# One subtraction of 2048 columns for the low part of a block of adj in the last pass, in place of two of 1024

## The chip, the core and the metric

The kernel runs on one core of a Trainium2 chip. The time is that of the device for one execution, in microseconds (us). The core's engines that matter here are TensorE (PE in the profile; PEld is its weight load), VectorE (DVE), ScalarE (ACT), and SyncE (SP), whose queue issues the transfers. Each engine works through its own instructions in the order in which they are written, and waits on semaphores that other engines raise.

## The reference

A graph network over 4096 nodes with 128 features each, and one 4096 x 4096 matrix `adj` that serves as every adjacency matrix:

```python
x = layernorm(x + relu(adj @ x @ kernel + bias))
u, v = x, v_node_feats
for _ in range(3):
    v = mlp(adj @ u, uv weights)      # three 128 x 128 layers with leaky_relu
    u = mlp(adj @ v, vu weights)
return layernorm(x + v)
```

So `adj` is multiplied with a 4096 x 128 matrix six times (the last `u` isn't used): six passes, each dependent on the one before. All of it is float32.

## The kernel before

`adj` (64 MB) doesn't fit on the chip and is read from memory again and again, in blocks of 512 x 512, that is 128 partitions x 2048 columns, 1 MB each. A block is used for the pass at hand ("finish") and, where the order allows it, for the start of the next pass too ("begin"), so passes 0 to 4 use most blocks twice. The last pass has nothing to begin: its 36 blocks are used once each, which makes it the stretch with the most loads for each product.

Precision comes from splitting. A float32 operand is written as a high part (rounded to the matmul's float32 format) and a low part (what is left), and a product is made of three matmuls: high x high, low x high, high x low. For each block of `adj`:

- SyncE loads it in two halves of 1024 columns (512 KB each) into `adj_raw`, a ring of 8 halves. It may load half h only when VectorE has finished with half h-8 (the wait on `adj_lo_ready` in `block.sync`, L492 issues the load).
- ScalarE copies each half to the high part (L613) as soon as TensorE has used up the block that lay in the target's place. There are 4 places in `adj_hi`/`adj_lo`, and in the last pass 2 more in the feature buffers that are no longer needed (`feat_hi`/`feat_lo` in the profile's rows at L613 and L742 are those).
- VectorE subtracts the high part from the raw half and writes the low part (L742), with one increment of `adj_lo_ready` a half.
- TensorE uses them: L878 (high x high), L885 (low features), L892 (low part of adj), 12 matmuls of 512 columns a block. The very last block has its own lines, L866 to L869.

Between these run the steps of the small network (MLP) of each finished group of 512 nodes, a "unit". In the last pass, for the row r of blocks that has just been finished: VectorE adds the two partial sums (`part`, L731), TensorE multiplies by the first weights (L825; L828 where nothing is to be added), ScalarE applies leaky_relu (`hid`, L507), TensorE the second layer (L811), ScalarE again, TensorE the third (L789), VectorE adds the bias (`pre`, L709), ScalarE applies leaky_relu (`post`, L507), and the normalisation follows: VectorE sum with x (L690), statistics (L626, L630), ScalarE square root (`std`, L538), VectorE reciprocal and shift (L665, L667), ScalarE the result (`resid`, L528), SyncE the store. Hidden layers in passes before the last one are split in high and low parts too (`in_lo` L722, `hid_lo` L717; TensorE L750 to L752).

The order of everything is fixed ahead of time by `Plan`, in ticks of one 128-column tile of a block (three matmuls). `steps` gives each MLP step its tick, `due` gives each half of a block the tick at which ScalarE and VectorE turn to it, in the last pass 20 ticks ahead of its use. In one tick an engine first issues the MLP steps and then the halves that are due. The rows of the last pass are done in the order 7, 0, 6, 5, 4, 3, 1, 2.

Of the kernel before, what the change touches and what calls it, by code (L numbers as in the profile page):

```python
# [4 lines left out]
F32 = mybir.dt.float32  # L5
F32R = mybir.dt.float32r
ALU = mybir.AluOpType
# [3 lines left out]
CHUNK = 512  # L11
# [6 lines left out]
PASSES = 6  # L18
RING = 4
SPARE = 2  # L20
RAW = 8
# [100 lines left out]
class Plan:  # L122
# [90 lines left out]
    def pieces_before(self, b, pieces):  # L213

        return TILES if b in self.first_spare else pieces

    def first_use(self, b):
        return next(n for n, of in enumerate(self.block) if of == b)
# [17 lines left out]
    def kind_of(self, u):  # L236
        return KINDS[self.units[u][0]]
# [42 lines left out]
def gnn_kernel(nc, x, adj, weights, bias_rows, out):  # L280
    C = x.shape[0]
    plan = Plan(C)
# [10 lines left out]
    with ctx:  # L293
        def sb(name, shape, dt=F32):
            return ctx.enter_context(nc.sbuf_tensor(name, shape, dt))
# [4 lines left out]
        def sem(name):  # L300
            return ctx.enter_context(nc.semaphore(name))

        adj_raw = sb("adj_raw", [P, RAW, HALF])
# [42 lines left out]
        adj_hi_ready = sem("adj_hi_ready")  # L346
        adj_lo_ready = sem("adj_lo_ready")
# [44 lines left out]
        def columns(chunk):  # L392
            return slice(chunk * CHUNK, (chunk + 1) * CHUNK)
# [61 lines left out]
        def split_block(adj, feat, b):  # L455

            k = plan.slot[b]
            return adj[:, k, :] if k < RING else feat[PASSES % 2][:, (k - RING) * BLOCK:(k - RING + 1) * BLOCK]

        def split_hi(b):  # L460
            return split_block(adj_hi, feat_hi, b)

        def split_lo(b):
            return split_block(adj_lo, feat_lo, b)
# [40 lines left out]
        def _(act):  # L505
# [7 lines left out]
            for t in range(plan.ticks + TAIL):  # L513
# [77 lines left out]
                if g is not None:  # L591
                    s, _, r = plan.groups[g]
                    act.wait_ge(half_used, plan.pieces_of(plan.closes[g]))
                    of = plan.unit_of(s, r)
                    if s and plan.summed(of):
                        if plan.in_parts(of):
                            act.wait_ge(in_lo_ready, plan.count_in_parts(of))
                        else:
                            act.wait_ge(hid1_done, deep(of) + 1)
                    act.activation(part_of(plan.node(s, r)), group_bank(g), ACT.Copy).then_inc(part_kept, 1)  # L600
# [17 lines left out]
        def _(dve):  # L618
# [26 lines left out]
            h = 0  # L645
            for t in range(plan.ticks + TAIL):
# [55 lines left out]
                if u is not None:  # L702
                    b = OUT_BIAS[kind_of(u)]
# [29 lines left out]
                while h < len(plan.loads) and plan.due[h] <= t:  # L733
                    b, i, pieces = plan.loads[h]
                    if b in plan.brings_x and i == 0:
                        c = plan.brings_x[b]
                        dve.wait_ge(x_hi_ready, plan.xs.index(c) + 1)
                        dve.tensor_tensor(feat_lo[0][:, columns(c)], resid[:, columns(c)],
                                          feat_hi[0][:, columns(c)].bitcast(F32), ALU.subtract).then_inc(x_lo_ready, 1)
                    slot = slice(i * CHUNK, (i + pieces) * CHUNK)  # L740
                    dve.wait_ge(adj_hi_ready, h + 1)
                    dve.tensor_tensor(split_lo(b)[:, slot], adj_raw[:, h % RAW, 0:pieces * CHUNK],  # L742
                                      split_hi(b)[:, slot].bitcast(F32), ALU.subtract).then_inc(adj_lo_ready, 1)
                    h += 1

        @block.tensor
        def _(pe):
# [173 lines left out]
```

## Time and profile before

| | us |
|---|---|
| median of three runs | 1170.84 (1170.68 to 1171.25) |
| the profiled execution | 1170.68 |
| its span, first to last instruction | 1168.8 |
| TensorE busy | 1154.0 (99%) |
| VectorE busy | 738.1 (63%) |
| ScalarE busy | 660.9 (57%) |
| L742 on VectorE, 488 halves | 577.0 |

The span is 1.9 us less than the time of the same execution. TensorE's granted clock is 0.999 over the span. In the page's 40 slices TensorE is at 9 tenths from the second to the last but one. VectorE is at 4 to 6 tenths in the middle and at 6 to 8 tenths in the last five, which are the last pass. An instruction's row gives its start and its duration. Where an engine stood idle before it, square brackets name for how long and who ended it. Two VectorE or ScalarE instructions in a row overlap in these rows by about 0.09 us, so the second starts a little before the first one's end.

### The profile page before, as it was taken

To read this page: it belongs to the slowest core of one execution; us is meant where nothing else is said; L and a number is where in the kernel's file an instruction comes from. 1 tells how busy PE (TensorE), PEld (TensorE's weight loads), DVE (VectorE), ACT (ScalarE), POOL (GpSimd) and SP (SyncE) were. 2 spreads that over 40 slices of the span, in tenths; PEclk is the share of its full clock that TensorE was granted. 3 is DMA by queue.
4 is the path that set the end of the run, shared out by engine and by line. 5 is a ranking of instruction groups with operands and counts; after the bars stand their busy time and mean duration, and the time that the engine had idled before them with its cause. 6 is when DMAs were issued, how large, how long until landed. Compare 5 with 4: busy or idle time off the path is not lost.

```text
span 1168.8 us, 13697 instructions
## 1 busy us (share of the span) xinstructions
PE 1154.0 (99%) x5236; PEld 953.2 (82%) x5236; DVE 738.1 (63%) x890; ACT 660.9 (57%) x809; POOL 0.2 (0%) x4
## 2 busy tenths in 40 slices
PE   7999999999999999999999999999999999999997
PEld 6888888888888888888888888888888888887776
DVE  7997676458564555555545746554566555678884
ACT  7765555346554555555444754554556444667874
POOL 0000000000000000000000000000000000000000
PEclk9999999999999999999999999999999999999999
DMA  9988785568366646555656736655665555589870
GB/s 383 406 302 321 247 271 191 206 215 288 125 205 210 216 161 224 189 184 180 216 180 216 250 116 223 207 179 178 207 225 184 195 200 214 188 296 362 297 261 36
DMA packets 72209, 261.60 MB, mean 224 GB/s; under 512 B 8016, under 2 KB 8656, under 8 KB 71120
## 3 DMA queue, kind: packets, MB, share of 16 engines
q1 hardware_dynamic: 72000, 260.61, 63.6%
q8 instruction: 41, 0.67, 0.2%
q14 instruction: 24, 0.20, 0.0%
q10 hardware_dynamic: 144, 0.13, 0.0%
HBM read 258.61 MB, written 2.10 MB: 223 GB/s over the span
## 4 chain that ended last, share of the span: by engine, by line
PE 93%; DMA 3%; DVE 2%; ACT 1%; issue 0%; SPq 0%; DVEq 0%; ACTq 0%
PE agg_ps L892 28%; PE agg_ps L885 28%; PE agg_ps L878 28%; PE pre_ps L789 4%; DMA adj_raw<-in_adj 3%; PE hid_ps L750 1%; PE hid_ps L752 1%; PE hid_ps L751 1%; DVE adj_lo L742 1%; ACT adj_hi L613 1%; PE hid_ps L811 1%; PE hid_ps L825 0%; ACT feat_hi L613 0%; DVE stats L626 0%; ACT resid L528 0%
## 5 line engine op out<-in xcount | busy, mean ns | idle before, releaser
L742 DVE TENSOR_TENSOR adj_lo<-adj_raw,adj_hi 128x1024 fp32r<-128x1024 f32 x464 | 548.1, 1221 | 226.4 <-ACT adj_hi L613 221.0
L878 PE MATMUL agg_ps<-adj_hi,feat_hi 128*128 128x512 f32 x1484 | 587.0, 396 | 7.5 <-ACT adj_hi L613 7.5
L885 PE MATMUL agg_ps<-adj_hi,feat_lo 128*128 128x512 f32 x1484 | 579.4, 390 | 0.0
L613 ACT ACTIVATE adj_hi<-adj_raw 128x1024 fp32r<-128x1024 f32 x464 | 468.3, 1052 | 86.0 <-PE agg_ps L892 72.4
L892 PE MATMUL agg_ps<-adj_lo,feat_hi 128*128 128x512 f32 x1484 | 458.8, 390 | 0.2 <-DVE adj_lo L742 0.2
L878 PEld LDWEIGHTS agg_ps<-adj_hi,feat_hi 128*128 128x128 f32 x1484 | 279.6, 188 | 66.4 <-issue 9.8
L885 PEld LDWEIGHTS agg_ps<-adj_hi,feat_lo 128*128 128x128 f32 x1484 | 279.5, 188 | 59.7 <-issue 2.4
L892 PEld LDWEIGHTS agg_ps<-adj_lo,feat_hi 128*128 128x128 f32 x1484 | 278.9, 188 | 59.6 <-DVE adj_lo L742 1.1
L507 ACT ACTIVATE hid<-hid_ps,params 128x512 f32<-128x512 f32 (+1 forms) x80 | 54.5, 681 | 61.0 <-PE hid_ps L752 50.6
L578 ACT ACTIVATE in_hi<-part 128x512 fp32r<-128x512 f32 x24 | 15.2, 634 | 110.4 <-DVE part L731 110.4
L507 ACT ACTIVATE post<-pre 128x512 f32<-128x512 f32 x39 | 24.6, 631 | 79.8 <-DVE pre L709 79.8
L709 DVE TENSOR_TENSOR pre<-pre_ps,b_row 128x512 f32<-128x512 f32 x47 | 32.4, 690 | 55.5 <-PE pre_ps L789 55.5
L731 DVE TENSOR_TENSOR part<-part,agg_ps 128x512 f32<-128x512 f32 (+1 forms) x31 | 20.6, 666 | 66.7 <-PE agg_ps L892 65.0
L789 PEld LDWEIGHTS pre_ps<-params,hid 128*128 128x128 f32 x380 | 49.9, 191 | 4.0
L789 PE MATMUL pre_ps<-params,hid 128*128 128x128 f32 x380 | 50.3, 275 | 0.0
L600 ACT ACTIVATE part<-agg_ps 128x512 f32<-128x512 f32 x30 | 17.9, 597 | 25.6 <-PE agg_ps L892 22.3
L742 DVE TENSOR_TENSOR feat_lo<-adj_raw,feat_hi 128x1024 fp32r<-128x1024 f32 x24 | 28.9, 1223 | 4.5 <-ACT feat_hi L613 4.1
L613 ACT ACTIVATE feat_hi<-adj_raw 128x1024 fp32r<-128x1024 f32 x24 | 24.8, 1056 | 9.0 <-PE agg_ps L892 8.9
L717 DVE TENSOR_TENSOR hid_lo<-hid,hid_hi 128x512 fp32r<-128x512 f32 x32 | 22.0, 687 | 11.9 <-ACT hid L507 11.9
L578 ACT ACTIVATE in_hi<-agg_ps 128x512 fp32r<-128x512 f32 x8 | 4.8, 598 | 41.5 <-PE agg_ps L892 41.5
L507 ACT ACTIVATE hid_hi<-hid_ps,params 128x512 fp32r<-128x512 f32 x32 | 21.9, 684 | 10.6 <-PE hid_ps L752 10.6
L722 DVE TENSOR_TENSOR in_lo<-agg_ps,in_hi 128x512 fp32r<-128x512 f32 x8 | 5.5, 691 | 35.2 <-ACT in_hi L578 35.2
(78 smaller groups left out, 382.3 us busy)
## 6 DMA issues: line engine op xcount, KB each, us to landing
adj_raw<-in_adj SPq DMA_DIRECT2D x472, 512.0 KB, 5.6
adj_raw<-in_adj SPq DMA_DIRECT2D x8, 1024.0 KB, 8.1
resid<-in_x SPq DMA_DIRECT2D x8, 256.0 KB, 8.1
out<-resid SPq DMA_DIRECT2D x7, 256.0 KB, 5.5
params<-in_weights SPq DMA_DIRECT2D x1, 386.0 KB, 4.7
b_row<-in_bias_rows SPq DMA_DIRECT2D x1, 128.0 KB, 5.6
out<-resid ACTq DMA_DIRECT2D x1, 128.0 KB, 2.1
out<-resid SPq DMA_DIRECT2D x1, 128.0 KB, 2.2
```

What stands on the lines that cost most here:

```text
L507: return act.activation(to, of, ACT.Prelu, alpha=SLOPE, **bias)
L578: act.activation(in_hi[:, :], agg(u), ACT.Copy).then_inc(in_hi_ready, 1)
L600: act.activation(part_of(plan.node(s, r)), group_bank(g), ACT.Copy).then_inc(part_kept, 1)
L613: act.activation(split_hi(b)[:, i * CHUNK:(i + pieces) * CHUNK], adj_raw[:, h % RAW, 0:pieces * CHUNK], ACT.Copy).then_inc(adj_hi_ready, 1)
L709: dve.tensor_tensor(by_tile(pre[:, own(u)]), by_tile(layer_bank(2, u)), b_row[:, b * P:(b + 1) * P].rearrange("p (j f) -> p j f", f=P) .to ...
L717: dve.tensor_tensor(hid_lo[:, :], hid1[:, :], hid_hi[:, :].bitcast(F32), ALU.subtract)\
L731: dve.tensor_tensor(agg(u), agg(u), agg_bank(u), ALU.add).then_inc(sum_kept, 1)
L742: dve.tensor_tensor(split_lo(b)[:, slot], adj_raw[:, h % RAW, 0:pieces * CHUNK], split_hi(b)[:, slot].bitcast(F32), ALU.subtract).then_inc ...
L789: last = pe.matmul(layer_bank(2, u)[:, k * P:(k + 1) * P], hid2[:, j * P:(j + 1) * P], w_raw[:, OUT_W[kind_of(u)], :], start=not biased, s ...
L878: pe.matmul(group_bank(g), feat_hi[feats][:, tile(src, i)], split_hi(b)[:, piece(i)], start=start, stop=False)
L885: pe.matmul(group_bank(g), feat_lo[feats][:, tile(src, i)], split_hi(b)[:, piece(i)], start=False, stop=False)
L892: last = pe.matmul(group_bank(g), feat_hi[feats][:, tile(src, k)], split_lo(b)[:, piece(k)], start=False, stop=stop and k == i)
```

## The change

In the last pass (blocks whose first use is in pass 5, 36 of them) VectorE does nothing at a block's first half. At the second half it waits until both high parts are there and makes the low part of the whole block in one subtraction of 2048 columns, and then raises `adj_lo_ready` by 2. Both raw halves lie side by side in the ring. Blocks of passes 0 to 4 are done as before, in two subtractions. ScalarE's, TensorE's and SyncE's programs are the same as before.

```diff
+    def low_at_once(self, b):
+        return self.order[self.first_use(b)][0] == PASSES - 1
...
+                    h += 1
+                    if plan.low_at_once(b):
+                        if i == 0:
+                            continue
+                        raw = adj_raw[:, (h - 2) % RAW:(h - 2) % RAW + 2, :].rearrange("p k f -> p (k f)")
+                        dve.wait_ge(adj_hi_ready, h)
+                        dve.tensor_tensor(split_lo(b), raw, split_hi(b).bitcast(F32), ALU.subtract)\
+                           .then_inc(adj_lo_ready, 2)
+                        continue
                     slot = slice(i * CHUNK, (i + pieces) * CHUNK)
-                    dve.wait_ge(adj_hi_ready, h + 1)
-                    dve.tensor_tensor(split_lo(b)[:, slot], adj_raw[:, h % RAW, 0:pieces * CHUNK],
+                    dve.wait_ge(adj_hi_ready, h)
+                    dve.tensor_tensor(split_lo(b)[:, slot], adj_raw[:, (h - 1) % RAW, 0:pieces * CHUNK],
                                       split_hi(b)[:, slot].bitcast(F32), ALU.subtract).then_inc(adj_lo_ready, 1)
-                    h += 1
```

VectorE's order at the turn of the passes, where the last unit of pass 4 goes through its MLP (`in_lo`, `hid_lo`), before:

```order
L722 TENSOR_TENSOR in_lo<-agg_ps,in_hi 128x512
L742 TENSOR_TENSOR adj_lo<-adj_raw,adj_hi 128x1024
L742 TENSOR_TENSOR feat_lo<-adj_raw,feat_hi 128x1024 x2
L717 TENSOR_TENSOR hid_lo<-hid,hid_hi 128x512
```

and after:

```order
L726 TENSOR_TENSOR in_lo<-agg_ps,in_hi 128x512
L750 TENSOR_TENSOR adj_lo<-adj_raw,adj_hi 128x2048
L750 TENSOR_TENSOR feat_lo<-adj_raw,feat_hi 128x2048
L721 TENSOR_TENSOR hid_lo<-hid,hid_hi 128x512
```

A first half that stood ahead of `in_lo` has moved behind it, so that four halves stand between `in_lo` and `hid_lo` in place of three.

VectorE's order where row 7's unit is normalised and row 6's sum follows (`post` to `part`), before:

```order
L709 TENSOR_TENSOR pre<-pre_ps,b_row 128x512
L742 TENSOR_TENSOR feat_lo<-adj_raw,feat_hi 128x1024
L742 TENSOR_TENSOR adj_lo<-adj_raw,adj_hi 128x1024
L690 TENSOR_TENSOR post<-post,resid 128x512
L626 BN_STATS stats<-post 128x6 x4
L630 BN_AGGR mean_var<-stats 128x2 x4
L742 TENSOR_TENSOR adj_lo<-adj_raw,adj_hi 128x1024 x2
L665 RECIPROCAL rstd<-std 128x4
L667 SCALAR_TENSOR_TENSOR shift<-mean_var,rstd 128x4
L742 TENSOR_TENSOR adj_lo<-adj_raw,adj_hi 128x1024
L731 TENSOR_TENSOR part<-part,agg_ps 128x512
```

and after:

```order
L713 TENSOR_TENSOR pre<-pre_ps,b_row 128x512
L750 TENSOR_TENSOR feat_lo<-adj_raw,feat_hi 128x2048
L694 TENSOR_TENSOR post<-post,resid 128x512
L630 BN_STATS stats<-post 128x6 x4
L634 BN_AGGR mean_var<-stats 128x2 x4
L750 TENSOR_TENSOR adj_lo<-adj_raw,adj_hi 128x2048
L669 RECIPROCAL rstd<-std 128x4
L671 SCALAR_TENSOR_TENSOR shift<-mean_var,rstd 128x4
L750 TENSOR_TENSOR adj_lo<-adj_raw,adj_hi 128x2048
L735 TENSOR_TENSOR part<-part,agg_ps 128x512
```

A first half that stood ahead of the sum with x (`post`) has moved behind the statistics.

VectorE's order where row 5's unit ends and row 4's sum follows, before:

```order
L709 TENSOR_TENSOR pre<-pre_ps,b_row 128x512
L742 TENSOR_TENSOR feat_lo<-adj_raw,feat_hi 128x1024 x2
L690 TENSOR_TENSOR post<-post,resid 128x512
L626 BN_STATS stats<-post 128x6 x4
L630 BN_AGGR mean_var<-stats 128x2 x4
L742 TENSOR_TENSOR adj_lo<-adj_raw,adj_hi 128x1024 x2
L665 RECIPROCAL rstd<-std 128x4
L667 SCALAR_TENSOR_TENSOR shift<-mean_var,rstd 128x4
L731 TENSOR_TENSOR part<-part,agg_ps 128x512
```

and after:

```order
L713 TENSOR_TENSOR pre<-pre_ps,b_row 128x512
L750 TENSOR_TENSOR feat_lo<-adj_raw,feat_hi 128x2048
L694 TENSOR_TENSOR post<-post,resid 128x512
L630 BN_STATS stats<-post 128x6 x4
L634 BN_AGGR mean_var<-stats 128x2 x4
L750 TENSOR_TENSOR adj_lo<-adj_raw,adj_hi 128x2048
L669 RECIPROCAL rstd<-std 128x4
L671 SCALAR_TENSOR_TENSOR shift<-mean_var,rstd 128x4
L735 TENSOR_TENSOR part<-part,agg_ps 128x512
```

Here every step keeps its place, and each pair of halves has become one instruction.

## Rows read from the trace of the kernel before

**Rows 1.** Busy time by stretch: PE, PEld, DVE, ACT, POOL, PEclk, DMA share, GB/s.

```profile
1040.00:1060.00 20.00, 20.00 (x93) 16.43 (x93) 19.16 (x18) 17.04 (x19) 0.00 (x0) 1.00 0.94 348
1100.00:1140.00 40.00, 39.80 (x176) 31.46 (x175) 35.78 (x53) 31.75 (x41) 0.00 (x0) 1.00 0.78 278
```

**Rows 2.** Group of L742 on the page: busy us, mean ns, idle before, releaser.

```profile
L742 DVE TENSOR_TENSOR adj_lo<-adj_raw,adj_hi 128x1024 fp32r<-128x1024 f32 x464 | 548.1, 1221 | 226.4 <-ACT adj_hi L613 221.0
```

**Rows 3.** Timeline of PE (start, duration, us): the last block's first matmul.

```profile
1155.63 0.28 PE L866 MATMUL agg_ps<-adj_hi,feat_hi 128*128 128x256 f32 x1
```

**Rows 4.** Timeline of all engines, turn of the passes.

```profile
1036.37 1.23 DVE L742 TENSOR_TENSOR adj_lo<-adj_raw,adj_hi 128x1024 fp32r<-128x1024 f32 x1 [0.26 <-ACT adj_hi L613]
...
1037.51 2.35 DVE L742 TENSOR_TENSOR feat_lo<-adj_raw,feat_hi 128x1024 fp32r<-128x1024 f32 x2
...
1040.43 0.69 DVE L717 TENSOR_TENSOR hid_lo<-hid,hid_hi 128x512 fp32r<-128x512 f32 x1 [0.57 <-ACT hid L507]
...
1041.27 0.47 PE L750 MATMUL hid_ps<-hid_hi,w_hi 128*128 128x512 f32 x1
```

**Rows 5.** Timeline of all engines, row 7's statistics and row 6's first layers.

```profile
1084.32 0.62 ACT L507 ACTIVATE post<-pre 128x512 f32<-128x512 f32 x1
1084.45 1.23 DVE L742 TENSOR_TENSOR adj_lo<-adj_raw,adj_hi 128x1024 fp32r<-128x1024 f32 x1 [1.26 <-ACT adj_hi L613]
...
1085.59 0.69 DVE L690 TENSOR_TENSOR post<-post,resid 128x512 f32<-128x512 f32 x1
...
1091.17 0.68 DVE L731 TENSOR_TENSOR part<-part,agg_ps 128x512 f32<-128x512 f32 x1
...
1092.00 1.10 PE L825 MATMUL hid_ps<-part,params 128*128 128x512 f32 x2 [0.35 <-DVE part L731]
...
1095.28 1.12 PE L811 MATMUL hid_ps<-hid,params 128*128 128x512 f32 x2 [0.34 <-ACT hid L507]
```

**Rows 6.** Timeline of all engines, row 5's second layer.

```profile
1113.26 0.66 ACT L507 ACTIVATE hid<-hid_ps,params 128x512 f32<-128x512 f32 x1
1114.43 1.02 PE L811 MATMUL hid_ps<-hid,params 128*128 128x512 f32 x2
```

**Rows 7.** Timeline of all engines, row 5's statistics and row 4's first layers.

```profile
1119.85 2.59 DVE L742 TENSOR_TENSOR feat_lo<-adj_raw,feat_hi 128x1024 fp32r<-128x1024 f32 x2 [0.45 <-ACT feat_hi L613]
...
1122.35 0.68 DVE L690 TENSOR_TENSOR post<-post,resid 128x512 f32<-128x512 f32 x1
...
1126.81 0.69 DVE L731 TENSOR_TENSOR part<-part,agg_ps 128x512 f32<-128x512 f32 x1
1126.92 1.65 ACT L528 ACTIVATE resid<-post,shift,rstd 128x128 f32<-128x128 f32 x4 [0.31 <-DVE shift L667]
...
1130.38 0.67 ACT L507 ACTIVATE hid<-hid_ps,params 128x512 f32<-128x512 f32 x1
...
1131.10 1.12 PE L811 MATMUL hid_ps<-hid,params 128*128 128x512 f32 x2 [0.20 <-ACT hid L507]
```

**Rows 8.** Timeline of all engines, row 4's statistics and row 3's first layer.

```profile
1138.01 1.22 DVE L742 TENSOR_TENSOR adj_lo<-adj_raw,adj_hi 128x1024 fp32r<-128x1024 f32 x1 [0.16 <-ACT adj_hi L613]
1139.16 0.69 DVE L690 TENSOR_TENSOR post<-post,resid 128x512 f32<-128x512 f32 x1
...
1141.08 0.65 DVE L731 TENSOR_TENSOR part<-part,agg_ps 128x512 f32<-128x512 f32 x1
...
1142.10 1.02 PE L825 MATMUL hid_ps<-part,params 128*128 128x512 f32 x2
```

**Rows 9.** Single loads and a split in the timelines of SP and ACT.

```profile
1033.12 0.33 SPq L492 DMA_DIRECT2D adj_raw<-in_adj  x1
...
1051.44 0.33 SPq L492 DMA_DIRECT2D adj_raw<-in_adj  x1
...
1059.12 1.06 ACT L613 ACTIVATE feat_hi<-adj_raw 128x1024 fp32r<-128x1024 f32 x1 [0.30 <-PE agg_ps L892]
```

**Rows 10.** All users of `adj_raw` from 1040 to 1060 us, its loads' landing times.

```profile
DMA to landing us min/median/max: 4.8/6.6/7.0
```

## The prediction

> **What bounds the kernel now.** I read the busy times by stretch first. TensorE is the engine at its limit. In the last pass it is busy 20.00 of 20 us and 39.80 of 40 us at a granted clock of 1.00, while VectorE has 19.16 of 20 and 35.78 of 40 [rows 1]. So any wait that is put on TensorE lengthens the run, since its matmuls come in a fixed order and none is skipped. A change on VectorE counts only where TensorE waits for it.
>
> Next comes the page's group for L742. A half takes 1221 ns, and VectorE idles 221 us in total before it until ScalarE's high part is there [rows 2]. VectorE is mostly ahead of its supply and not behind it.
>
> Then I looked at how early the low parts are. The last half starts at 1138.01 and ends at 1139.23 [rows 8], and TensorE takes up the last block at 1155.63 [rows 3]. That is 16.4 us of lead, so low parts that come one or two us later are not missed by the matmuls that read them.
>
> What has no such lead are the MLP steps. They stand in the same order on VectorE and ScalarE, behind the low parts. TensorE's waits in the last pass are all of that kind: 0.35 us for the sum `part`, 0.34 and 0.20 us for `hid` [rows 5, 7]. At other places the step comes only just in time.
>
> **The price of one merged subtraction.** 512 columns take 0.69 us (`hid_lo` [rows 4]) and 1024 take 1.22 us [rows 2], so 512 more cost 0.53 us and 2048 come to 1.22 + 2 x 0.53 = 2.28 us. Two halves in a row took 2.35 us [rows 4], so the second starts 2.35 - 1.22 = 1.13 us after the first. The next instruction starts about 0.09 us before the end of the one ahead. The merged one therefore holds VectorE for some 2.20 us, against 2 x 1.13 = 2.26 us. This saves about 0.06 us a block where both high parts are ready, or 36 x 0.06 = 2.2 us of VectorE's time in all. No row shows 2048 columns. If the fixed part were lost and only the data rate counted, it would be 2 x 1.07 = 2.14 us, and if nothing were saved 2.26 us. I take 2.20, which the two shapes give by a straight line.
>
> **What the merge delays.** Where VectorE waits for ScalarE, it did the first half while the second one's high part was still being made. Now it starts both when the second is ready. The step behind came 1.14 us after the second half's start (1138.01 to 1139.16 [rows 8]) and now comes 2.20 us after it, so it is 1.06 us late (0.99 to 1.12 with the bounds above). I followed this through each MLP unit between VectorE, ScalarE and TensorE.
>
> - Turn of the passes [rows 4]. The first merged one starts at 1036.37, the second at 1038.57, and `hid_lo` at 1040.77 in place of 1040.43. The gap of 0.57 us, in which it waited for ScalarE, covers the rest. `hid_lo` ended at 1041.12, and TensorE started L750 0.15 us later at 1041.27, so it has nothing in hand. TensorE: +0.34 us.
> - Row 6 [rows 5]. Here the order helps. The half at 1084.45 goes behind the statistics, and L690 can start once ScalarE's `post` is done, at 1084.32 + 0.62 = 1084.94, about 0.6 us earlier than 1085.59. Behind it stand two whole blocks in place of three halves, 2.20 - 1.13 = 1.07 us more. The sum `part` comes about 0.42 us later, and TensorE's wait of 0.35 us grows to 0.77. But ScalarE, which waited for the shift in this chain, is 0.6 us earlier, and with TensorE itself 0.42 us later the wait of 0.34 us at 1095.28 goes. Net: +0.08 us.
> - Row 5 [rows 6]. The same pattern as for row 4 in the next point. VectorE's shift is 1.02 us late, ScalarE waits for it, and its `hid` at 1113.26 comes 1.02 us late. From the start of such a `hid` to TensorE's start it takes 0.72 us (1130.38 to 1131.10 [rows 7]), so it was ready at 1113.98 for a matmul that went at 1114.43, with 0.45 us to spare. Net: +0.57 us.
> - Row 4 [rows 7]. Of the pair at 1119.85 the second half starts at 1119.85 + 2.59 - 1.23 = 1121.21. The merged one starts then, and L690 moves from 1122.35 to 1123.41. The next pair needs no wait and gives back about 0.04, so the shift is 1.02 us late. L528 had been waiting for that shift, 0.31 us. Everything behind it on ScalarE is back to back up to `hid` at 1130.38, for which TensorE already waited 0.20 us. Net: +1.02 us. The sum `part` is 1.02 us late as well, at 1126.81 + 0.69 + 1.02 + 0.15 = 1128.67 for L825. That lies in the same stretch of TensorE's order, ahead of L811, which now has to wait until 1132.12 anyway, so it adds nothing.
> - Row 3 [rows 8]. L690 and the sum `part` are 1.06 us late. `part` ended at 1141.73 and TensorE could have started 0.15 us later, as it did behind the `part` of [rows 5], at 1141.88. It started at 1142.10, so 0.22 us are to spare. Net: +0.84 us.
> - Rows 1 and 2 and the end: no low part is left behind 1139.23, and nothing changes but that all is shifted.
>
> Sum: 0.34 + 0.08 + 0.57 + 1.02 + 0.84 = 2.85 us, or 2.5 to 3.2 us with the merged one at its bounds. The delays add up, since ScalarE's splits wait for TensorE to free a place and so shift with it. The profiled execution took 1170.68 us with a span of 1168.8. It becomes 1173.5 us. The median of the runs is 0.16 us above it, which gives 1173.7. I forecast 1173.6.
>
> **The loads.** The raw halves come free later too, and SyncE's loads, which wait for them in order, start later. The worst is the half whose place let SyncE issue at 1033.12 [rows 9]. Its low part is now done at 1036.37 + 2.28 = 1038.65, and the load goes 5.5 us later, just ahead of the stretch in which the DMA engines are 94% busy [rows 1]. The load issued at 1051.44 is split at 1059.12, 7.68 us later, and the slowest of these lands in 7.0 [rows 9, 10]. So 0.7 us are to spare there, and 0.34 more since TensorE's shift moves the split. One lost transfer of 512 KB at 348 GB/s is 1.5 us. It uses up the spare and makes a few splits late by about half a us. These have the 16 us of lead above. I cost it at nothing, and if the MLP steps behind those splits are hit, at up to 1.5 us.
>
> **A rule that cuts both ways.** The rows show VectorE 89 to 96% busy in the last pass and yet waiting for ScalarE before several of its halves [rows 1, 4, 5, 7, 8]. The Trainium skill, Perfetto Trace Analysis, section "Optimizing Scalar/DVE Operations", says that larger operations help throughput if the engine is saturated, and that breaking instructions up may let work finish sooner where the engine isn't saturated but leaves bubbles on others. By its first half the change would gain, which is the second rival below. By its second half it would lose, as in my sum, and the brackets of the rows speak for that.
>
> **Rivals.**
>
> 1. VectorE counts as the bottleneck of the last pass, and the 0.06 us a block come through. The places where VectorE has a backlog (the pairs without a bracket) and the reordering of row 6, which pulls a chain forward by 0.6 us, speak for it. Against it are the brackets ahead of L742 in four of the groups. What TensorE can get back is only what it waits for: 0.35 + 0.34 + 0.20 = 0.89 us, so at best 1169.8 us and more likely 1170.5. It decides if the steps behind merged blocks come no later than before. This is the case that isn't slower.
> 2. The delays are real, but only part of them reaches TensorE, because an order of waits that I have wrong leaves more to spare in one or two of the chains of rows 5, 4 and 3. If the term of 1.02 or 0.84 drops out, 1.8 to 2.0 us are left: 1172.6 us.
> 3. The raw ring becomes the bound as well. The late load at the turn pushes the splits, and ScalarE's `hid` steps between 1060 and 1080 us come late for TensorE, by up to 1.5 us on top: 1174 to 1175 us. The spare of 0.7 us speaks against it being large, and the DMA share of 94% speaks for it.
>
> That the change doesn't do what it says is excluded by the order, which shows 128x2048 in VectorE's program.
>
> **Chances and range.** A difference of 0.2% (2.3 us) is about what can be told from no change, so my sum lies just above that border. I give the forecast 0.50, with its own range of 1172.8 to 1174.3, and 0.07 of that falls below 1173.2. Rival 1 gets 0.20, of which 0.02 is for a gain of more than 0.2% that no term of mine explains. Rival 2 gets 0.15 and rival 3 gets 0.15. Slower: 0.43 + 0.15 = 0.58. Same: 0.07 + 0.18 + 0.15 = 0.40. Faster: 0.02. For the range I leave out the lower half of rival 1 and the far end of rival 3: 1170.8 to 1175.0.
>
> **What the profile of the changed kernel would show.** VectorE's new L750 should stand there 36 times with 128x2048 at 2.28 us. TensorE should show new idle time before L825 and L811 (their new line numbers) of rows 5, 4 and 3, released by DVE `part` or ACT `hid`, of about 0.6, 1.0 and 0.8 us, about 0.3 us before the second layer at the turn (L750 in the rows of before), and the wait before the `hid` layer of row 6 gone. The time before 1036 us should be the same as before. The forecast is wrong if these waits aren't there (rival 1 or 2), or if ScalarE's splits between 1042 and 1062 us are released by DMA landings in place of TensorE (rival 3).

## The result, and the profile after

| | before | after |
|---|---|---|
| median of 10 runs, us | 1170.73 (1170.51 to 1171.25) | 1173.91 (1173.70 to 1174.16) |
| span of the profiled execution, us | 1168.8 | 1172.3 |

The kernel became 3.18 us slower. The ratio of the runs is 1.0027, with a 95% interval of 1.0017 to 1.0037. The forecast was 1173.6 us, with 1172.8 to 1174.3 as its own range and 1170.8 to 1175.0 as the whole one.

The page's groups of the merged subtraction (busy us, mean ns, idle before and who ended it):

```profile
L750 DVE TENSOR_TENSOR adj_lo<-adj_raw,adj_hi 128x2048 fp32r<-128x2048 f32 x24 | 54.8, 2285 | 13.6 <-ACT adj_hi L617 13.6
...
L750 DVE TENSOR_TENSOR feat_lo<-adj_raw,feat_hi 128x2048 fp32r<-128x2048 f32 x12 | 27.5, 2290 | 7.0 <-ACT feat_hi L617 7.0
```

There are 24 + 12 = 36 of them with 2285 to 2290 ns each, as the straight line through the two shapes gave (2.28 us). VectorE's busy time over the whole span fell from 738.1 to 735.1 us, and yet the kernel is slower.

Busy time by stretch, columns as in [rows 1], which these two rows answer:

```profile
1040.00:1060.00 20.00, 19.32 (x90) 15.84 (x89) 18.07 (x11) 16.71 (x19) 0.00 (x0) 1.00 0.97 340
...
1100.00:1140.00 40.00, 38.73 (x168) 29.79 (x167) 33.62 (x39) 30.85 (x40) 0.00 (x0) 1.00 0.85 293
```

TensorE now idles 0.7 and 1.3 us where it idled 0.0 and 0.2. VectorE does less in both, and the clock is the same.

What TensorE waited for, from 1020 us to the end (us in total, times, longest):

```profile
PE hid_ps L837 <- DVE part L735: 2.0, 3, 0.8
PE hid_ps L823 <- ACT hid L511: 0.7, 2, 0.5
PE hid_ps L762 <- DVE hid_lo L721: 0.7, 1, 0.7
PE agg_ps L801 <- ACT hid L511: 0.6, 1, 0.6
```

The last of the four stood there before the change too, in the tail after the last product. The other three sum to 3.4 us, where before there were 0.9 us (the brackets in [rows 5, 7]). All of them are steps of the small network, and none is for a low part of adj.

The turn of the passes, answering [rows 4], in the timeline of all engines (start us, duration us):

```profile
1037.07 2.29 DVE L750 TENSOR_TENSOR adj_lo<-adj_raw,adj_hi 128x2048 fp32r<-128x2048 f32 x1 [0.68 <-ACT adj_hi L617]
...
1039.28 2.28 DVE L750 TENSOR_TENSOR feat_lo<-adj_raw,feat_hi 128x2048 fp32r<-128x2048 f32 x1
...
1041.48 0.68 DVE L721 TENSOR_TENSOR hid_lo<-hid,hid_hi 128x512 fp32r<-128x512 f32 x1
...
1042.31 0.47 PE L762 MATMUL hid_ps<-hid_hi,w_hi 128*128 128x512 f32 x1 [0.68 <-DVE hid_lo L721]
```

A merged one holds VectorE for 2.21 us (1037.07 to 1039.28), as predicted. But the first starts after an idle time of 0.68 us, where the 1024 columns of before waited 0.26.

Rows 6, 5, 4 and 3 on TensorE, answering [rows 5 to 8]:

```profile
1093.42 1.10 PE L837 MATMUL hid_ps<-part,params 128*128 128x512 f32 x2 [0.75 <-DVE part L735]
...
1096.19 1.02 PE L823 MATMUL hid_ps<-hid,params 128*128 128x512 f32 x2
...
1115.81 1.13 PE L823 MATMUL hid_ps<-hid,params 128*128 128x512 f32 x2 [0.21 <-ACT hid L511]
...
1130.19 1.10 PE L837 MATMUL hid_ps<-part,params 128*128 128x512 f32 x2 [0.53 <-DVE part L735]
...
1133.64 1.12 PE L823 MATMUL hid_ps<-hid,params 128*128 128x512 f32 x2 [0.52 <-ACT hid L511]
...
1145.54 1.10 PE L837 MATMUL hid_ps<-part,params 128*128 128x512 f32 x2 [0.76 <-DVE part L735]
```

TensorE's matmuls stand in the same order in both programs, so the start of the same matmul in the two traces tells where the time goes. Before the last pass the new trace lies 0.28 us behind, a difference that arises in the first 45 us, where both do the same work. The traces of the ten kernels below lie there between 0.18 us ahead of the kernel before and 0.18 us behind it. The matmul at 1041.27 then comes 1.04 us later (1042.31), row 6's L811 at 1095.28 comes 0.91 later, row 5's at 1114.43 comes 1.38 later, row 4's at 1131.10 comes 2.54 later, row 3's at 1142.10 comes 3.44 later, and there it stays up to the end.

| place | predicted, us | measured, us |
|---|---|---|
| turn of the passes | +0.34 | 1.04 - 0.28 = +0.76 |
| row 6, and up to row 5's sum | +0.08 | 0.77 - 1.04 = -0.27 |
| row 5 | +0.57 | 1.38 - 0.77 = +0.61 |
| row 4 | +1.02 | 2.54 - 1.38 = +1.16 |
| row 3 | +0.84 | 3.44 - 2.54 = +0.90 |
| sum | +2.85 | +3.16 |

(The 0.77 is where the matmuls just ahead of row 5's L825 stand.) The terms are taken from start to start of the matmul that waits, so a pair that takes longer behind its wait counts in the next term: 0.10 of row 4's 1.16 us is row 5's second layer, which took 1.13 us in place of 1.02. And 0.25 of row 5's 0.61 us arises at its first layer, L825. It starts 0.17 us later than the matmuls ahead of it would have it (1111.72 before, 1112.66 after), 0.15 us behind the end of its `part`, and its pair takes 0.08 us longer. The prediction leaves this step out for row 5, and the profile shows no bracket there.

The chain behind it at row 4, which is the one to read closely, VectorE's timeline answering [rows 7]:

```profile
1122.76 2.29 DVE L750 TENSOR_TENSOR feat_lo<-adj_raw,feat_hi 128x2048 fp32r<-128x2048 f32 x1 [0.75 <-ACT feat_hi L617]
1124.97 0.69 DVE L694 TENSOR_TENSOR post<-post,resid 128x512 f32<-128x512 f32 x1
...
1129.36 0.69 DVE L735 TENSOR_TENSOR part<-part,agg_ps 128x512 f32<-128x512 f32 x1
```

Before, the sum with x started 1.14 us after the second half did (1121.21 to 1122.35). Now it starts 2.21 us after the merged one. `part` moved from 1126.81 to 1129.36, 2.55 us. The split that released the merged one was itself 1.48 us behind, with TensorE (ScalarE's start moved from 1120.12 to 1121.60), so 1.07 us of that are new. The prediction has 1.02.

### The profile page after: what moved, and what is told of

Same layout as the page of the kernel before. It is cut to its first block, busy times and chain, and to the rows that moved or that the text cites. A ratio compares the mean times of both kernels' runs of the same rounds, so it can differ in the third digit from the quotient of the medians.

```text
span 1172.3 us, 13697 instructions
## 1 busy us (share of the span) xinstructions
PE 1154.9 (99%) x5236; PEld 952.7 (81%) x5236; DVE 735.1 (63%) x854; ACT 660.9 (56%) x809; POOL 0.2 (0%) x4
## 4 chain that ended last, share of the span: by engine, by line
PE 91%; DMA 3%; DVE 3%; ACT 2%; issue 1%; SPq 0%; DVEq 0%; ACTq 0%
PE agg_ps L904 28%; PE agg_ps L897 27%; PE agg_ps L890 27%; PE pre_ps L801 4%; DMA adj_raw<-in_adj 3%; PE hid_ps L762 1%; PE hid_ps L764 1%; PE hid_ps L763 1%; DVE adj_lo L755 1%; ACT adj_hi L617 1%; PE hid_ps L823 1%; DVE adj_lo L750 1%; ACT resid L532 0%; DVE stats L630 0%; PE hid_ps L837 0%
## 5 line engine op out<-in xcount | busy, mean ns | idle before, releaser
L755 DVE TENSOR_TENSOR adj_lo<-adj_raw,adj_hi 128x1024 fp32r<-128x1024 f32 x416 | 491.3, 1221 | 214.1 <-ACT adj_hi L617 209.2
L750 DVE TENSOR_TENSOR adj_lo<-adj_raw,adj_hi 128x2048 fp32r<-128x2048 f32 x24 | 54.8, 2285 | 13.6 <-ACT adj_hi L617 13.6
L735 DVE TENSOR_TENSOR part<-part,agg_ps 128x512 f32<-128x512 f32 (+1 forms) x31 | 20.6, 666 | 66.7 <-PE agg_ps L904 65.0
L750 DVE TENSOR_TENSOR feat_lo<-adj_raw,feat_hi 128x2048 fp32r<-128x2048 f32 x12 | 27.5, 2290 | 7.0 <-ACT feat_hi L617 7.0
```

What stands on the lines that cost most here:

```text
L735: dve.tensor_tensor(agg(u), agg(u), agg_bank(u), ALU.add).then_inc(sum_kept, 1)
L750: dve.tensor_tensor(split_lo(b), raw, split_hi(b).bitcast(F32), ALU.subtract)\
L755: dve.tensor_tensor(split_lo(b)[:, slot], adj_raw[:, (h - 1) % RAW, 0:pieces * CHUNK], split_hi(b)[:, slot].bitcast(F32), ALU.subtract).th ...
```

## The experiments

Theory A is that of the prediction: a merged subtraction makes the short MLP step behind it late, and TensorE waits for that step at a few places. Theory B puts the loss on the raw halves and low parts, which come free in pairs and later (the third rival). Theory C puts it on the wide instruction itself. Each kernel was timed beside the kernel before on the same chip, and each difference below is to the median of those runs. The interval of each ratio is about 1.05 us to either side, so differences of less than that (+0.73, +0.15, +0.09, -0.34, -0.99, +0.69 below) are not told from nothing by the times alone. What carries the reading there is the place in the trace at which TensorE's matmuls move.

**The turn alone, and all but the turn.** The merged form in 9 blocks or in 27.

```diff
-        return self.order[self.first_use(b)][0] == PASSES - 1
+        return self.order[self.first_use(b)][0] == PASSES - 1 and b <= 216   # the other kernel: b > 216
```

> Merged only for the first 9 blocks of the last pass (blocks 208 to 216, up to the turn of the passes), halves for the other 27. Theory A (a merged subtraction makes the MLP step behind it late, and TensorE waits at single places): the turn alone costs what the changed kernel's trace shows there, +0.8 us in TensorE's place in its order (0.7 us of wait before hid_lo's matmul), so 1171.4 to 1171.6 us; the predicted term of 0.34 would give 1171.1. No new wait later. Theory B (late loads: the raw ring frees its halves late at the turn, and all later steps suffer): most of the 3.2 us is here, 1173 us or more.

> Merged only for the last 27 blocks (217 to 243), halves up to the turn. Theory A: the terms of rows 6, 5, 4 and 3 are left, -0.2 + 0.6 + 1.15 + 0.9 = 2.4 us by the changed kernel's trace: 1173.1 us, with waits of TensorE for part (rows 6, 4, 3) and hid (rows 5, 4) as in the changed kernel, and no wait at the turn. Theory B: under 1 us is left, 1171.5 us or less.

Measured: 1171.56 us against 1170.83, so +0.73 (ratio 1.0007, 0.9998 to 1.0016), and 1173.30 us, so +2.47 (1.0021, 1.0012 to 1.0030). The two parts sum to 3.20 us where the whole change costs 3.18. TensorE's waits of the first kernel:

```profile
PE hid_ps L762 <- DVE hid_lo L721: 0.7, 1, 0.7
PE agg_ps L801 <- ACT hid L511: 0.6, 1, 0.6
PE hid_ps L823 <- ACT hid L511: 0.5, 2, 0.3
PE hid_ps L837 <- DVE part L735: 0.4, 1, 0.4
```

The turn's wait is the only new one. TensorE's matmuls move by 0.76 us there and by no more than 0.02 afterwards. The loads went as late as in the changed kernel, and two splits waited 1.0 us in total for them, at no cost. So theory A holds in both kernels, and the late loads at the turn aren't the cause.

**Two late halves in place of the wide one.**

```diff
-                        dve.tensor_tensor(split_lo(b), raw, split_hi(b).bitcast(F32), ALU.subtract)\
-                           .then_inc(adj_lo_ready, 2)
+                        for k in range(2):
+                            dve.tensor_tensor(split_lo(b)[:, k * HALF:(k + 1) * HALF], raw[:, k * HALF:(k + 1) * HALF],
+                                              split_hi(b)[:, k * HALF:(k + 1) * HALF].bitcast(F32), ALU.subtract)\
+                               .then_inc(adj_lo_ready, 1)
```

> The same order and the same waits as the changed kernel (nothing at the first half, both at the second), but two subtractions of 1024 columns in place of one of 2048. Theory A: what costs is that the first half's work is put behind the second half's wait. The pair holds VectorE for 2.27 us in place of 2.21, so each step behind is as late as with the merged one or 0.05 us later: 1173.9 to 1174.2 us. Rival C (the wide instruction itself is what costs, by a later start or a longer run than two halves): most of the loss goes, 1170.7 to 1171.5 us.

Measured: 1173.88 us, +3.05 (1.0025, 1.0015 to 1.0034). The wide instruction isn't needed for the loss. It is enough that the first half's work stands behind the second half's wait, and theory C falls. Nor are late loads needed: in this kernel's trace no split of the last pass waits for a load, and the loss is there. The sum is a little under the +3.18 of the wide one in spite of the 0.06 us that each pair takes longer, because the turn is cheaper here. VectorE's timeline at the turn:

```profile
1036.54 2.36 DVE L751 TENSOR_TENSOR adj_lo<-adj_raw,adj_hi 128x1024 fp32r<-128x1024 f32 x2 [0.26 <-ACT adj_hi L617]
1038.82 2.35 DVE L751 TENSOR_TENSOR feat_lo<-adj_raw,feat_hi 128x1024 fp32r<-128x1024 f32 x2
1041.09 0.69 DVE L721 TENSOR_TENSOR hid_lo<-hid,hid_hi 128x512 fp32r<-128x512 f32 x1
```

The idle time before the pair is 0.26 us again, and the two pairs hold VectorE for 2.28 and 2.27 us.

**Merged where no step waits behind.** 24 blocks merged, 12 in halves.

```diff
-        return self.order[self.first_use(b)][0] == PASSES - 1
+        return self.order[self.first_use(b)][0] == PASSES - 1 \
+            and b not in (211, 212, 223, 224, 228, 231, 232, 234, 237, 238, 242, 243)
```

> Merged for 24 of the 36 blocks; the 12 that stand ahead of an MLP step for which TensorE waits or nearly waits (211, 212, 223, 224, 228, 231, 232, 234, 237, 238, 242, 243) stay in halves. Theory A: no step that TensorE needs is late, and with the order at row 6 a little better than before, 1170.3 to 1170.9 us. Theories B and C (two thirds of the merged blocks are left, and the raw ring is freed late just as often): two thirds of the loss, 1172.8 us.

Measured: 1170.98 us, +0.15 (1.0002, 0.9993 to 1.0011). Two thirds of the merging costs nothing that can be told, and no gain can be told either, although it saves VectorE time. It lies 0.1 us above the expected range. The gain at row 6 isn't there, since block 227's merged subtraction still stands with both halves of 228 between the statistics and `part`, and TensorE waited 0.8 us for row 6's `part`.

**The release late, the steps not.**

```diff
-                    dve.tensor_tensor(split_lo(b)[:, slot], adj_raw[:, h % RAW, 0:pieces * CHUNK],
-                                      split_hi(b)[:, slot].bitcast(F32), ALU.subtract).then_inc(adj_lo_ready, 1)
+                    last = dve.tensor_tensor(split_lo(b)[:, slot], adj_raw[:, h % RAW, 0:pieces * CHUNK],
+                                      split_hi(b)[:, slot].bitcast(F32), ALU.subtract)
+                    if plan.order[plan.first_use(b)][0] < PASSES - 1:
+                        last.then_inc(adj_lo_ready, 1)
+                    elif i:
+                        last.then_inc(adj_lo_ready, 2)
```

> The kernel before (36 blocks of the last pass in halves, each at its old place and with its old wait), only that the first half raises no semaphore and the second raises it by 2. So TensorE and SyncE hear of a block's low parts as late as with a merged one, but no step behind is late. Theory A (late MLP steps are the whole cost): 1170.6 to 1171.0 us, no wait of TensorE beyond those of before. Theory B (raw halves and low parts that come free in pairs cost): 1172 us or more.

Measured: 1170.72 us against 1170.63, +0.09 (1.0001, 0.9992 to 1.0010). SyncE and TensorE learn of each block in one step of 2, and it costs nothing that can be told. This run tests only the release in pairs. The merged subtraction also ends about 1.07 us later than the second half did, which is not in it. That part is covered by the turn alone and by the two late halves, where the loads cost nothing. Together the runs settle theory B for the changed kernel.

**The wide one with an increment of 1.**

```diff
-                           .then_inc(adj_lo_ready, 2)
+                           .then_inc(adj_lo_ready, 1)
...
+    def lows(self, h):
+        first = next(k for k, (b, i, _) in enumerate(self.loads) if self.low_at_once(b))
+        return h + 1 if h < first else first + (h - first) // 2 + 1
```

The waits of SyncE and TensorE on `adj_lo_ready` go by `plan.lows` here.

> The changed kernel, but the merged subtraction raises the semaphore by 1, with the counts that SyncE and TensorE wait for adapted. In the changed kernel's trace each merged subtraction has its wait as an instruction of its own (EVENT_SEMAPHORE) and starts 0.10 us after ScalarE's part, once 0.45, where a subtraction of before starts 0.03 after it. If the step of 2 is what splits the wait off, the wait goes back into the subtraction, which starts 0.03 us after ScalarE, and TensorE's wait at the turn falls from 0.7 to 0.35 us: 1173.3 to 1173.6 us. If the wide shape splits it off, nothing changes: 1173.9 us.

Measured: 1173.36 us, +2.73 (1.0022, 1.0013 to 1.0031), 0.45 us less than the changed kernel's +3.18. VectorE's timeline at the turn:

```profile
1036.47 2.29 DVE L755 TENSOR_TENSOR adj_lo<-adj_raw,adj_hi 128x2048 fp32r<-128x2048 f32 x1 [0.26 <-ACT adj_hi L622]
1038.67 2.29 DVE L755 TENSOR_TENSOR feat_lo<-adj_raw,feat_hi 128x2048 fp32r<-128x2048 f32 x1
1040.88 0.69 DVE L726 TENSOR_TENSOR hid_lo<-hid,hid_hi 128x512 fp32r<-128x512 f32 x1
```

The wait of 0.68 us is back at 0.26, and TensorE waits 0.3 us here in place of 0.7. The same matmul moves by 0.34 us over this place, which is the predicted term to the digit.

**VectorE's low parts 2 ticks later in the order,** with the merged form and with halves.

```diff
-                while h < len(plan.loads) and plan.due[h] <= t:
+                while h < len(plan.loads) and plan.due[h] + (
+                        2 if plan.order[plan.first_use(plan.loads[h][0])][0] == PASSES - 1 else 0) <= t:
```

> The changed kernel, with VectorE turning to the low parts of the last pass 2 ticks (1.36 us of matmuls) later in its order, so that MLP steps of the same ticks go ahead of them. TensorE still has over 10 us of lead on the low parts. Theory A: the late steps are the whole cost and go: 1170.0 to 1171.0 us, and TensorE's waits at the turn and for rows 5, 4 and 3 are gone. Theory B (late release of the raw ring, here 1.4 us later still): 1174 us or more.

> The kernel before in halves, with the same 2 ticks of lag for VectorE's low parts in the last pass. Theory A: TensorE's waits of 0.35, 0.34 and 0.20 us of before can go as well, 1169.9 to 1170.7 us, and level with or up to 0.3 us under the merged one with lag. Theory B: slower than before, 1171.5 us or more.

Measured: merged 1170.29 us, -0.34 (0.9997, 0.9988 to 1.0006), and halves 1169.64 us, -0.99 (0.9991, 0.9982 to 1.0000). Both go the way of theory A: with the MLP steps ahead of the low parts the merged form is no slower than the kernel before. The halves came out 0.26 us under their expected range. The last section has why. The merged form is 0.65 us behind the halves with the same lag, which is within the interval, but its trace shows a loss of that size. Two rows of its waits are not in the kernel before at all:

```profile
ACT adj_hi L617 <- DMA adj_raw<-in_adj: 2.9, 6, 1.4
...
ACT feat_hi L617 <- DMA adj_raw<-in_adj: 1.8, 4, 1.2
```

ScalarE's splits now wait 4.7 us in total for loads, and TensorE for a `hid` behind them:

```profile
1067.78 1.13 PE L823 MATMUL hid_ps<-hid,params 128*128 128x512 f32 x2 [0.61 <-ACT hid L511]
```

The matmuls move by 0.77 us at this place against the kernel before. So the third rival of the prediction exists, but only once the raw halves are kept longer than the change itself keeps them. In the changed kernel the splits waited 0.8 + 0.4 us for loads, and no MLP step was hit: between the turn and row 6 its matmuls don't move.

**Further the same way.** Both with halves: ScalarE's splits 1 tick later as well, and VectorE's lag at 4 ticks. VectorE's loop is edited as above, with 4 for 2 in the second kernel. ScalarE's loop in the first:

```diff
-                while h < len(plan.loads) and plan.due[h] <= t:
+                while h < len(plan.loads) and plan.due[h] + (
+                        1 if plan.order[plan.first_use(plan.loads[h][0])][0] == PASSES - 1 else 0) <= t:
```

> Halves with 2 ticks of lag on VectorE, and 1 tick of lag on ScalarE's splits of the last pass too, so that ScalarE's hid steps of a tick go ahead of splits. What TensorE still waits for with the lag on VectorE alone is one hid of 0.3 us. Theory A: that goes, 1169.3 to 1169.6 us. Against it: later splits hold later low parts and raw halves, and if the ring counts (theory B), 1170 us or more.

> Halves with 4 ticks (2.7 us) of lag on VectorE. Theory A: the MLP steps are all ahead already with 2 ticks, nothing is left to gain, 1169.6 us. Theory B (raw halves free late): ScalarE's splits wait for loads and its hid steps with them, 1170 to 1171.5 us.

Measured: 1168.70 us, -2.00 (0.9981, 0.9972 to 0.9990), and with 4 ticks 1171.39 us against 1170.70, +0.69 (1.0009, 1.0000 to 1.0018). The first is the fastest of all, 5.2 us under the changed kernel. It came out 0.6 us better than the best that was expected, since the expectation priced row 6's wait for `hid` at its bracket of 0.3 us. Against halves with VectorE's lag alone the matmuls gain 0.60 us there, and another 0.15 at the turn. All that TensorE waits for in its last pass:

```profile
PE agg_ps L789 <- ACT hid L507: 0.6, 1, 0.6
```

That is the wait in the tail, which every kernel here has. With 4 ticks the ring decides in the trace, which is of a short run (1170.80 us; the runs go from 1170.78 to 1173.68, and what the longest lost is in no trace). ScalarE's splits waited 2.4 + 2.1 us for loads, and TensorE stood 0.95 us before a `hid`:

```profile
1068.06 1.12 PE L811 MATMUL hid_ps<-hid,params 128*128 128x512 f32 x2 [0.95 <-ACT hid L507]
```

## Why the prediction was right, and where it was off

- **TensorE is the bound, and only its waits count.** Right. VectorE's busy time fell by 3.0 us and the kernel grew by 3.18. The kernel that merges 24 blocks away from the tight steps lies 0.15 us above before, less than can be told. The "89 to 96% busy" of VectorE holds for the two stretches of [rows 1] only. From 1060 to 1080 us it was busy 16.03 of 20 us, so it had more idle time than the prediction says.
- **The merged one takes 2.28 us and holds VectorE for 2.20.** Right: 2285 to 2290 ns, and 2.21 us from start to start.
- **The step behind is 1.06 us late.** Slightly low. In the changed kernel a merged one that waits starts 0.10 us after ScalarE's part in place of 0.03, so the step is 2.21 + 0.07 - 1.14 = 1.14 us late.
- **The turn, +0.34.** This term was mis-sized. It measured +0.76, since the merged one started 0.42 us later behind ScalarE's part than the half of before (0.45 in place of 0.03). The run with an increment of 1 took this away and left +0.34. That the semaphore's step would matter was in none of the cases.
- **Row 6, +0.08.** The mechanism was right, with L825's wait at 0.75 us (0.77 predicted) and the one before L811 gone. It measured -0.27, since a wait that goes also takes away what its first matmul costs beyond the bracket (last section).
- **Rows 5, 4 and 3, +0.57, +1.02, +0.84.** Right, each 0.04 to 0.14 low. The 0.08 us of the third point and the same cost beyond the bracket are about this size. Row 5's `part`, which the sum doesn't follow, took 0.25 of the 0.61 us, but `hid` comes behind it and sets the total.
- **The loads, costed at nothing.** Right as to the cost. But the sign that the prediction names for its third rival was there: four splits, at 1056.35, 1057.62, 1058.87 and 1060.15 us, were released by landings and not by TensorE, after 0.58, 0.21, 0.18 and 0.21 us of idle time. The spare of 0.7 us was used up, as the prediction says in its working, and the sign tells only that the ring is tight, not that TensorE pays. From 1040 to 1060 us the median load landed in 6.3 us (6.6 before [rows 10]), the slowest in 7.8, and the splits' waits for loads, 1.2 us in total, reached no step that TensorE needs. The run with the late release shows no cost of the release in pairs.
- **Rival 1 (not slower, as larger instructions save VectorE time),** which the prediction's paragraph on the rule calls the second rival, would have needed a VectorE without idle time before its subtractions. The first half of the rule quoted there from the Trainium skill, Perfetto Trace Analysis, "Optimizing Scalar/DVE Operations", does not apply here: VectorE waited 20.6 us for ScalarE before the 36 merged ones. Its second half, that breaking instructions up may end work sooner where an engine that isn't saturated leaves bubbles on another, agrees with these runs: halves against merged are 3.18 us apart as written, and 0.65 with 2 ticks of lag. But the size is not what counts: two late halves cost 3.05 us. What ends work sooner is that the first half starts before the second one's high part is there.
- **Rival 2 (part of the lateness doesn't reach TensorE).** None of the terms dropped out.
- **The sum.** 2.85 against 3.18. The errors at the turn (+0.42) and at row 6 (-0.35) nearly cancel, so that the sum comes this close is in part luck. That rows 5, 4 and 3 came out at the right places and nearly the right sizes is not.

## What to carry to other kernels

Merging two instructions on an engine with idle time moves the first one's work behind the second one's wait. The price is not the engine's busy time. It is how late the next short step in its queue comes for the engine that bounds the kernel, and it can be read step by step from the time to spare at each. If bulk work and latency-bound steps share an in-order queue, put the steps ahead and let the bulk work lag as far as its buffers allow. That gained 2.0 us here with 2 ticks on VectorE and 1 on ScalarE. With halves and a lag on VectorE alone, 2 ticks gave -0.99 us and 4 ticks +0.69, since the load ring then makes the splits wait.

## What the runs showed of the hardware that was not expected

**An instruction that raised its semaphore by 2 had its wait split off.** In the changed kernel's trace the waits of the 36 merged ones are instructions of their own in VectorE's queue:

```profile
L749 DVEq EVENT_SEMAPHORE  x36: 21/21/21, 1020.9 to 1140.5; - x36
```

In the kernel with the late release, where 36 subtractions of only 1024 columns raise by 2, they are there as well:

```profile
L741 DVEq EVENT_SEMAPHORE  x36: 21/21/21, 1020.7 to 1138.2; - x36
```

In the kernel with the wide subtraction and an increment of 1 there are none. So the increment does it and not the width. (VectorE has such instructions at other lines in every kernel. At the line of the low parts only these kernels and those with the same merged instruction have them.) A split wait made the subtraction start 0.10 us after ScalarE's part (which ended at 1117.96 + 1.06 = 1119.02 for a start at 1119.12) in place of 0.03 (1137.98 for 1138.01 before the change [rows 8]), and once, at the turn, 0.45 us after it (1035.57 + 1.05 = 1036.62 for 1037.07).

The 0.45 goes with the place in VectorE's instruction list. The turn alone and the merged one with lag have it at the same subtraction. The kernel with the late release has it elsewhere, behind a half of adj (ScalarE's part ended at 1026.85 + 1.06 = 1027.91):

```profile
1028.36 1.23 DVE L742 TENSOR_TENSOR adj_lo<-adj_raw,adj_hi 128x1024 fp32r<-128x1024 f32 x1 [0.56 <-ACT adj_hi L613]
```

Its subtraction behind `in_lo` starts 0.10 us after ScalarE. In all four traces the late one is the 832nd of the instructions that the trace has for VectorE, with its split wait as the 831st. In the kernel before the 832nd is a subtraction too (the half at 1036.37), with its wait inside, and starts 0.03 us after ScalarE. So both are needed, the split wait and this place, and a change that moves VectorE's list by one instruction may move the late start to where it costs nothing. That it fell on the turn, where TensorE has nothing in hand, was chance. What is special about the place stays open. Whether the compiler or the instruction's format asks for the split, these runs don't tell.

**A wait of TensorE costs more than its bracket.** The first pair of matmuls behind a wait takes 1.10 to 1.13 us, where the same pair without one takes 1.02 [rows 5, 6, 8]. And the bracket itself is short. It counts from the end of the matmul before in the trace, while a 512-column matmul that doesn't wait starts some 0.17 us before that end (rows of 0.39 us each follow every 0.22 to 0.23 us). So row 3's wait of 0.76 us moved the matmuls by 0.90, and row 6's second layer, which lost a wait of 0.34, gained 0.51, and 0.10 more in its second matmul. Halves with 2 ticks of lag lose two brackets of 0.35 and 0.20 us, and the matmuls gain 1.06. The longer pair goes with its weights. Row 4's first layer behind its wait for `part`, whose row ends at 1129.36 + 0.69 = 1130.05:

```profile
1130.16 0.30 PEld L837 LDWEIGHTS hid_ps<-part,params 128*128 128x128 f32 x2 [0.92 <-issue]
```

The weight load starts only 0.03 us ahead of its matmul (1130.19), where other loads in these traces start 0.2 us ahead of theirs. That this is the cause of the 0.08 us was not tried by itself.
